# The first weight and activation arrays of a gated LoRA feed-forward layer, laid out so that each transfer reads one unbroken stretch of HBM

## The reference

```python
hidden_i = einsum('bsd,fd->bsf', x, wi)
hidden_i += 2.0 * einsum('bsr,fr->bsf', einsum('bsd,rd->bsr', x, common_wi_a), common_wi_b)
hidden_i += expert_lora(x, ids, experts_wi_a, experts_wi_b)      # rows of the id's expert
hidden_i = relu(hidden_i)
hidden_o = einsum('bsf,df->bsd', hidden_i, wo)
hidden_o += 2.0 * einsum('bsr,dr->bsd', einsum('bsf,rf->bsr', hidden_i, common_wo_a), common_wo_b)
hidden_o += expert_lora(hidden_i, ids, experts_wo_a, experts_wo_b)
return x + hidden_o
```

## Time and profile before

| what | value |
|---|---|
| median of 3 runs | 127.63 us (126.83 to 127.8) |
| profiled execution | 127.72 us, of which the span from first to last instruction is 125.9 us |
| PE busy | 117.1 us, 93% of the span |
| DVE, ACT, POOL busy | 36%, 37%, 40% |
| mean granted TensorE clock | 0.973 of full |
| DMA | 14.67 MB, mean 116 GB/s |

### The profile page before, as it was taken

The page is one execution under the profiler, slowest core; times in us unless marked ns, Lnnn a source line. Parts: engine busy times, 40 slices in busy tenths (PEclk is TensorE's granted clock), DMA queues, the critical chain, the costliest instruction groups (busy, mean ns, idle before and its releaser), DMA issues.

```text
span 125.9 us, 1926 instructions
## 1 busy us (share of the span) xinstructions
PE 117.1 (93%) x728; PEld 105.8 (84%) x728; DVE 45.7 (36%) x85; ACT 46.7 (37%) x96; POOL 50.7 (40%) x65
## 2 busy tenths in 40 slices
PE   6649999999969999999999999999999999999971
PEld 6427888988858999978888999978889999999960
DVE  0238306685649302242444322242446022222221
ACT  3336009892667544231334444123334111111120
POOL 7007703888888637835021737824000020232000
PEclk9975699999999999999999999999999999999999
DMA  3899840699920101113885001115200011101112
GB/s 108 213 366 379 228 158 0 226 376 380 380 111 0 34 0 47 44 42 82 277 294 198 0 3 42 42 42 172 73 0 0 0 34 33 35 30 39 47 42 83
DMA packets 7708, 14.67 MB, mean 116 GB/s; under 512 B 946, under 2 KB 4706, under 8 KB 7570
## 3 DMA queue, kind: packets, MB, share of 16 engines
q1 hardware_dynamic: 7408, 14.14, 32.4%
q10 hardware_dynamic: 290, 0.39, 1.4%
HBM read 12.44 MB, written 2.10 MB: 115 GB/s over the span
## 4 chain that ended last, share of the span: by engine, by line
PE 85%; DMA 5%; DVE 3%; ACT 3%; SPq 1%; issue 1%
PE bank_h L520 28%; PE bank_o L574 19%; PE bank_h L574 19%; DMA x_raw<-in_xt 5%; PE bank_o L520 4%; PE bank_h L541 4%; PE bank_low L531 3%; PE bank_t L581 1%; PE bank_h L589 1%; DVE low_stack L406 1%; PE bank_low L520 1%; PE bank_t L520 1%; ACT low_stack L334 1%; PE bank_t L554 1%; PE bank_o L589 1%
## 5 line engine op out<-in xcount | busy, mean ns | idle before, releaser
L520 PE MATMUL bank_h<-xT,wiT 128*128 128x512 f32 x156 | 43.0, 417 | 4.1 <-ACT xT L321 1.6
L520 PEld LDWEIGHTS bank_h<-xT,wiT 128*128 128x128 f32 x156 | 29.8, 200 | 10.9 <-ACT xT L321 1.9
L574 PE MATMUL bank_h<-wcat,hid 128*128 128x272 f32 x192 | 26.1, 291 | 0.0
L574 PE MATMUL bank_o<-wcat,hid 128*128 128x272 f32 x192 | 25.5, 290 | 0.0
L574 PEld LDWEIGHTS bank_h<-wcat,hid 128*128 128x128 f32 x192 | 24.9, 188 | 0.0
L574 PEld LDWEIGHTS bank_o<-wcat,hid 128*128 128x128 f32 x192 | 24.7, 188 | 0.0
L406 DVE SCALAR_TENSOR_TENSOR hid<-bank_h,hid 128x512 fp32r<-128x512 f32 x26 | 17.2, 687 | 17.6 <-ACT hid L338 17.6
L338 ACT ACTIVATE hid<-bank_h 128x512 fp32r<-128x512 f32 x26 | 14.7, 598 | 19.8 <-PE bank_h L541 19.8
L244 POOL TENSOR_TENSOR bi_stack<-bi_raw,bi_stack 32x1024 fp32r<-32x1024 f32 x6 | 14.3, 2385 | 6.7 <-ACT bi_stack L354 6.7
L406 DVE SCALAR_TENSOR_TENSOR lo_stack<-bank_t,lo_stack 16x128 fp32r<-16x128 f32 x16 | 4.5, 282 | 25.6 <-ACT lo_stack L348 25.6
L348 ACT ACTIVATE lo_stack<-bank_t 96x128 fp32r<-96x128 f32 x16 | 4.3, 272 | 19.6 <-PE bank_t L581 19.6
(11 more groups left out here) (60 smaller groups left out, 104.9 us busy)
## 6 DMA issues: line engine op xcount, KB each, us to landing
bi_raw<-in_rec_bi SPq DMA_DIRECT2D x8, 512.0 KB, 5.8
x_raw<-in_xt SPq DMA_DIRECT2D x8, 256.0 KB, 5.6
x_res<-in_xn SPq DMA_DIRECT2D x4, 512.0 KB, 5.6
out<-o_sb SPq DMA_DIRECT2D x16, 128.0 KB, 1.7
p_raw<-in_rec_p SPq DMA_DIRECT2D x8, 160.0 KB, 5.8
wo_raw<-in_wot SPq DMA_DIRECT2D x1, 1024.0 KB, 6.0
wi_raw<-in_wit SPq DMA_DIRECT2D x1, 512.0 KB, 7.4
bo_raw<-in_rec_bo SPq DMA_DIRECT2D x8, 48.0 KB, 4.1
```

Source lines behind the costliest of these rows:

```text
L520: nc.tensor.matmul(bank[:, :], wiT[sw][:, m, k, :], xT[sx][step % 2][:, k, :], start=(i == 0), stop=False)
L574: last = nc.tensor.matmul(out_bank[t][:, 0:WIN], hid[sh][step % 2][:, m, tok], wcat[sw][:, m, win], start=(m == 0 and i == 0), stop=(m == ...
```

## The change

`wi` becomes four arrays in HBM, one for each piece, and `x` is laid out as [step, half, 128 partitions, 512]. Each of the transfers of wi and x then reads one unbroken stretch of HBM. The rows that go to the partitions keep their sizes (2 KB for x; 1, 1, 2 and 4 KB for wi) and follow one another without gaps. Destinations, queues, the order of issue, semaphores and all arithmetic stay.

```diff
-def conditional_ffn(nc, xt, xn, ids, wit, wot, rec_p, rec_bi, rec_bo, aoc, boc, out):
+def conditional_ffn(nc, xt, xn, ids, wi_pieces, wot, rec_p, rec_bi, rec_bo, aoc, boc, out):
...
-                    sp.dma_start(x_raw[:, k, :], xt[step, :, k, :]).then_inc(x_in[k], 16)
+                    sp.dma_start(x_raw[:, k, :], xt[step, k, :, :]).then_inc(x_in[k], 16)
...
-                sp.dma_start(wi_raw[:, a:z, :, :], wit[:, a:z, :, :]).then_inc(wi_in[i], 16)
+                sp.dma_start(wi_raw[:, a:z, :, :], wi_pieces[i]).then_inc(wi_in[i], 16)
...
-            sp.dma_start(x_raw[:, 0, :], xt[0, :, 0, :]).then_inc(x_in[0], 16)
+            sp.dma_start(x_raw[:, 0, :], xt[0, 0, :, :]).then_inc(x_in[0], 16)
             load_wi(0)
-            sp.dma_start(x_raw[:, 1, :], xt[0, :, 1, :]).then_inc(x_in[1], 16)
+            sp.dma_start(x_raw[:, 1, :], xt[0, 1, :, :]).then_inc(x_in[1], 16)
...
-                act.dma_start(wi_raw[:, a:z, :, :], wit[:, a:z, :, :]).then_inc(wi_in[i], 16)
+                act.dma_start(wi_raw[:, a:z, :, :], wi_pieces[i]).then_inc(wi_in[i], 16)
...
-    xt = x.reshape(Q, PAIR * S, KD, P).transpose(0, 3, 2, 1)
+    xt = x.reshape(Q, PAIR * S, KD, P).transpose(0, 2, 3, 1)
...
-    for name, a in (("xt", xt), ("xn", xn), ("ids", ids), ("wit", wit), ("wot", wot), ("rec_p", rec_p), ("rec_bi", rec_bi),
+    for name, a in (("xt", xt), ("xn", xn), ("ids", ids), ("wi_0", wit[:, :1]), ("wi_1", wit[:, 1:2]), ("wi_2", wit[:, 2:4]),
+                    ("wi_3", wit[:, 4:]), ("wot", wot), ("rec_p", rec_p), ("rec_bi", rec_bi),
```

More of the change, by code:

```diff
@@ L18 @@
 ALPHA = 2.0
-def conditional_ffn(nc, xt, xn, ids, wit, wot, rec_p, rec_bi, rec_bo, aoc, boc, out):
+def conditional_ffn(nc, xt, xn, ids, wi_pieces, wot, rec_p, rec_bi, rec_bo, aoc, boc, out):
     P = 128
-    STEPS, _, KD, T = xt.shape
+    STEPS, KD, _, T = xt.shape
     TT, D = xn.shape[2:]
-    MF = wit.shape[1]
-    F = MF * P
-    E = rec_bi.shape[0]
+    E, _, F = rec_bi.shape
+    MF = F // P
     R = rec_bo.shape[1] // 3
@@ L691 @@
     args.append(nc.dram_tensor("out_0", (Q, P, PAIR * U, D), F32, kind="ExternalOutput").ap())
-    conditional_ffn(nc, *args)
+    conditional_ffn(nc, *args[:3], args[3:7], *args[7:])
     result = run_bass_kernel_spmd(nc, [arrays], core_ids=[0])
```

## The result

| | before | changed |
|---|---|---|
| median of 4 runs | 127.72 us (126.83 to 128.42) | 124.94 us (122.83 to 126.61) |
| profiled execution, time and span | 127.72 and 125.9 us | 123.62 and 121.8 us |
| ratio | | 0.9652, 95% interval 0.9536 to 0.9768 |

The change makes the kernel faster. The four times of the changed kernel are 122.83, 123.62, 126.25 and 126.61; every ratio in this document leaves out the executions more than 1.5% above their kernel's fastest, here the last two, in which TensorE's clock was low for a while (mean granted 0.986 against 1.0), so the medians of all executions, given beside it, are the more cautious measure. They differ by 2.78 us, or 2.2%; the forecast gain was 2.33 us.

The account below looks back on a forecast made before the run. PE, busy 93% of the span, was taken as the bound, so transfers count only where it idles at the start. Stream 1.13 plus clock 1.2 gives 2.33 us off 127.63: 125.3 us, range 123.0 to 128.7.

Parts of the forecast that it names:

- the slump costs 1.13 us: Start, 3 to 5 us: transfers at 143 and not 330 GB/s; unbroken reading lands x half 1 1.13 us earlier.
- the other part of its bound: Some engines lag 1.9 us before x half 1 lands; about 1.4 from the same cause would make the gain 2.5 us.
- I take 1.2 us: 27 matmuls after x half 1: TensorE's clock gives back 1.2 us, a little under half of the 2.77 us lost.
- the upper part of the bound (2.77): 27 matmuls after x half 1: the whole half-clock loss returns if the clock does not fall; lower bound -0.56 us.
- the idling brings the fall: Start: PE stood still twice before its clock fell; less idling may make it rise earlier or not fall, up to 2.77 us.
- The sum: Whole kernel: 1.13 + 1.2 = 2.33 us off the median of 127.63 gives 125.3 us.
- The signs: Start: near 300 GB/s, piece 0 before 4.7, x half 1 by about 7.1, PE's first two waits some 1.7 us together.
- What is late next: Behind the front: `low_in` has 5.3 us of cover, other waits move with PE, so the front's gain reaches the end.
- the loads of x in later steps: Steps 1 to 3: the six x loads are hidden, so they cost and give nothing.
- Rival A: Loads of wi and x: the rows' distance does not matter, the slump stays, 127.6 us; chance 0.32.
- B2: Start: the stream gains 1.13 us, the clock gives nothing; 0.56 to 1.13 us gained, 127.1 to 126.5; chance 0.10.
- C: x half 1 and piece 2 of wi: unbroken reading slows to 139 GB/s, 2.2 us more, 129.8 or 128.7; chance 0.16.

Follow-up runs that it names:

- padded kernel: The kernel before, wi still one array, each partition's row padded from 8 to 9 KB: 125.01 us, ratio 0.9704.
- 16 KB: The kernel before with each partition's row of wi padded from 8 to 16 KB: 126.31 us, against 127.07 us beside it; no ratio given.
- filled kernel before: The kernel before plus matmuls on zeros where TensorE idles, 3 more at the warm-up and 7 ahead of x half 1: 125.47 us, ratio 0.9871.
- wi alone: The change without its lines on x: wi in four unbroken arrays, x halves still interleaved: 124.25 us, ratio 0.9681.
- pieces 0 and 1: The kernel before with only these pieces of wi unbroken in own arrays, pieces 2 and 3 read from the whole wi: 127.32 us, ratio 0.9943.
- four arrays: The kernel before with each piece of wi reading its own copy of the whole wi, rows still 8 KB apart: 126.86 us, ratio 0.9981.
- both changes: The changed kernel with pieces 1 and 2 of wi issued by SP behind x half 1, no longer on ACT's queue: 122.88 us, ratio 0.9648.
- x alone: The kernel before with only x laid out in halves, wi still one array: 126.63 us, ratio 0.9947.
- pieces 0 and 1 at 2 KB steps: The changed wi, four arrays with pieces 2 and 3 unbroken, but the 1 KB rows of the first two 2 KB apart: 124.88 us, ratio 0.977.

## Why the prediction was right

**The front.** The step "the slump costs 1.13 us" had the right mechanism and too small a size: 1.80 us. By the bytes, 1024 KB were through at 6.4 us before and at 5.2 now (128 and 365 GB/s for 2 us each make 986 thousand bytes; the other 63 take 0.2 us at 332), which is the 1.13 us, nearly. The rest is lag: the last part of x half 1 came 1.9 us behind that count before, and comes 1.3 us behind it now. (The count takes all that moved for those 1024 KB, though other loads are under way by then; it is an estimate.) The prediction had named this as the other part of its bound, up to 2.5 us, and taken none of it. The padded kernel shows the same (through at 5.14, landed at 6.05, lag 0.9), while every kernel with the whole of wi at 8 or 16 KB steps lags by 1.9 to 2.4 us. So a third of the 1.9 us of lag, or half by the padded kernel, comes from the same cause.

**The clock.** "I take 1.2 us" was 2.33 us in the profiled execution, where the clock did not fall. In two of the four it was low for some time, and those are about 3 us longer. So 1.2 us is near the mean over the executions, and the upper part of the bound (2.77) is what one without the fall gets. That the idling brings the fall was an argument in the prediction. The filled kernel before shows it for this gap: with the gaps filled, none of its four executions loses the time. The profiles agree: the clock fell after waits for x half 1 of 1.35 us (wi alone), 1.62 (before), 2.40, 2.43 and 2.74 (16 KB, pieces 0 and 1, four arrays), and did not after 0.98 (changed), 0.67 and 0.61 (both changes, 9 KB). When the clock comes up first is another matter, and the idling does not settle it (last section).

**The sum.** 2.33 forecast, 2.78 us by the medians of all executions and 4.1 by the profiled pair. That the time of 125.3 came so near to 124.94 is partly luck: a front that was put too small and a clock that fell in half of the executions offset each other.

**The signs.** Those of being right came: 365 GB/s where it asked for some 300, piece 0 taken up at 4.15 (before 4.7), x half 1 landed at 6.46 (by 7.1), and PE's two first waits 0.98 us together and not 1.7.

**What is late next.** Right: `low_in`, `up_lora` and the wait near 37 us hid nothing and took nothing; the 108 us behind the front are the same in all rows of the table. That the loads of x in later steps give nothing agrees with x alone, which cannot be told from no change (0.9947).

**Rival A** (the distance doesn't matter) is out: 9 KB against 8 KB in one array is 3% by the ratio. The Trainium skill, "DMA: Bandwidth & Descriptors", section Latency and other measured facts, lists steps from 512 KiB upwards and has nearly the full rate at 512 KiB. Taken on to smaller steps, which the page itself does not do, the change would have given nothing; here a step of 8 KB with rows of 1 and 2 KB cost 1.8 us at the front, and the measurement decides. The remedy that the same section names, padding by a few KiB or laying tiles out contiguously, did work, and 1 KB of padding was enough. **B2** (the front gains, the clock does not) fits the changed kernel's two longer executions, whose mean granted clock was 0.986, but neither was profiled. **C** is out: with the change x half 1 landed at 6.46 us and not after 9.5, and the stretch that C had priced at 139 GB/s ran at 332.

## What to carry to other kernels

When early transfers show busy engines and a low rate, look at the step from row to row of the source, not only at the size of the row; padding the host array by one row's worth is a one-line test. Before that, count what is ahead of the transfer that is waited for: taking 384 KB out of its way gave at least as much as speeding everything up, and the two gains did not add. And where TensorE idles at the start of a kernel, a delay of the operands can be paid twice, once as waiting and once in clock; a few matmuls on zeros in the gap tell the two apart. They do not rule out that the clock comes up late.

## What was not expected of the hardware

- Rows 8 KB apart slow a load even at 1 to 2 KB a row and 1 MB in all: 143 GB/s from 3 to 5 us (160 in a second profile of the layout), against 343 at 9 KB.
- The granted clock of a page does not count what lies before its first change. The kernel with x alone reads 1.00 in every stretch, yet its matmuls on half 1 of x take as long as at half clock, and only later run at full speed:

```profile
8.86 7.21 PE bank_h L520 x21
16.07 1.36 PE bank_o L520 x6
```

  21 matmuls at the pace of the second row (0.23 us each) would take 4.8 us, not 7.2. The first change of the clock in this trace is a rise, at 13.43 us. A mean of 1.0 is therefore no proof of a full clock at the start; a row's time divided by its matmuls tells. So do the zeros of the filled kernel before: the same matmul takes 0.23 us in its warm-up and 0.12 in the gap, with a granted clock of 1.00 in the rows of both.
- Little idling is not enough for a full clock. With pieces 0 and 1 at 2 KB steps TensorE waits only 0.33 us for half 1, less than in the changed kernel, and still works on it at half clock, at 0.43 us a matmul, until the trace's first rise, at 10.32 us; the changed kernel's clock is up at 5.87. What decides when it first comes up no run here tells.

```profile
6.94 6.68 PE L519 MATMUL bank_h<-xT,wiT 128*128 128x512 f32 x21 [0.33 <-ACT xT L320]
```

- Unbroken rows do not rule a slump out (166 GB/s at 0.56 busy in the kernel with both changes).
